# Attention scores from fp16 high and low parts in one 96-row contraction, with the next image's column scan and first turned tiles ahead of the first score

## What is computed

```python
Bx, Cx, Hx, Wx = x.shape
...
H, D = (6, 32)
WIN = 33
PAD = (WIN - 1) // 2
```

## Time and profile before

| | |
|---|---|
| median of the runs | 2979.17 us (2968.48 to 2982.03) |
| the profiled execution's own time | 2979.13 us |
| its span | 2977.3 us |
| PE busy | 2501.1 us (84%) |
| DVE busy | 1862.8 us (63%) |
| ACT busy | 1173.2 us (39%) |
| POOL busy | 810.9 us (27%) |
| fp32 score products, L1644 | 304.4 us, 704 instructions |
| mask products, L1647 | 118.6 us, 352 instructions |

### The profile page before, as it was taken

How to read it: one execution, slowest core, us unless ns; L and a number is a source line. 1 busy time by engine, 2 the same in 40 slices (tenths; PEclk the granted TensorE clock), 3 DMA queues, 4 the chain that set the end, 5 groups by cost and what they waited for, 6 DMA issues and landing times. The chain is left out here.

```text
span 2977.3 us, 50620 instructions
## 1 busy us (share of the span) xinstructions
PE 2501.1 (84%) x18147; PEld 1875.5 (63%) x18147; DVE 1862.8 (63%) x5249; ACT 1173.2 (39%) x3443; POOL 810.9 (27%) x656
## 2 busy tenths in 40 slices
PE   1349797889899899989898998989898998988697
PEld 0237575667676676767676776767676766766364
DVE  5346465766666665666676666656666666665454
ACT  0015343444443534444443435344443435353122
POOL 0000021323241313323232313233232413232444
PEclk9759697999999999899998999998999999998898
DMA  1540021334224233334333242433342242424664
GB/s 42 76 145 14 13 64 29 97 68 104 72 50 123 40 113 58 95 74 102 72 93 83 43 129 34 122 54 99 68 106 70 50 124 30 119 47 118 148 163 101
DMA packets 272442, 242.24 MB, mean 81 GB/s; under 512 B 208988, under 2 KB 250174, under 8 KB 261568
## 3 DMA queue, kind: packets, MB, share of 16 engines
q1 hardware_dynamic: 211456, 147.61, 18.5%
q0 software_dynamic: 50880, 52.59, 10.8%
q10 hardware_dynamic: 9856, 38.80, 4.1%
HBM read 133.73 MB, written 73.59 MB: 70 GB/s over the span
## 5 line engine op out<-in xcount | busy, mean ns | idle before, releaser
L1596 PE MATMUL PSUM<-XT,WB 128*128 128x512 f16 x2010 | 530.6, 397 | 22.7 <-DMA META<-slots 17.3
L740 POOL DMA_INDIRECT out_dram<-Y,META x228 | 359.0, 1575 | 565.8 <-DVE Y L1136 443.7
L886 ACT ACTIVATE PSPT<-PSUM,NMX 94x126 f32<-94x126 f32 x1056 | 367.1, 358 | 368.2 <-PE PSUM L1656 188.5
L854 ACT ACTIVATE HF<-PSUM,WB 128x512 f32<-128x512 f32 x402 | 274.1, 686 | 509.4 <-PE PSUM L1596 508.5
L1614 PE MATMUL PSUM<-WB,HHI 128*128 128x192 f16 x1608 | 403.4, 251 | 46.7 <-DVE HLO L1112 45.3
L1615 PE MATMUL PSUM<-WB,HHI 128*128 128x192 f16 x1608 | 402.2, 250 | 0.0
L1616 PE MATMUL PSUM<-WB,HLO 128*128 128x192 f16 x1608 | 402.0, 250 | 0.0
L1109 DVE TENSOR_SCALAR HHI<-HF 128x512 f16<-128x512 f32 x402 | 177.6, 442 | 328.5 <-ACT HF L854 326.5
L1596 PEld LDWEIGHTS PSUM<-XT,WB 128*128 128x128 f16 x2010 | 199.0, 102 | 189.9 <-issue 33.5
L1644 PE MATMUL PSUM<-KBD,QT 128*94 128x378 f32 x704 | 304.4, 516 | 9.1 <-ACT PSPT L886 7.5
L1112 DVE SCALAR_TENSOR_TENSOR HLO<-HF,HHI 128x512 f16<-128x512 f32 x402 | 278.4, 692 | 13.8
(11 more groups left out here) (276 smaller groups left out, 4412.6 us busy)
## 6 DMA issues: line engine op xcount, KB each, us to landing
WB<-weights SPq DMA_DIRECT2D x67, 1600.0 KB, 6.9
XR<-in_x ACTq DMA_DIRECT2D x16, 768.0 KB, 5.3
out_dram<-X ACTq DMA_DIRECT2D x32, 384.0 KB, 2.9
weights<-WB ACTq DMA_DIRECT2D x4, 1600.0 KB, 6.5
GUP<-TGU SPq DMA_DIRECT2D x256, 8.0 KB, 1.8
slots<-XROW,IDX POOLq DMA_INDIRECT x256
out_dram<-Y,META POOLq DMA_INDIRECT x228, 3.6
HF<-in_w ACTq DMA_DIRECT2D x6, 384.0 KB, 4.7
```

Source lines behind the costliest of these rows:

```text
L740: pool.indirect_dma_start(out[:, :], bass.IndirectOffsetOnAxis(row, 0), Y[:, wslot(i, j), q, :], None, bounds_check=B * T + BS - 1, oob_is ...
L854: act.activation(HF[:, k % 2, :], PSUM[:, 4 + k % 2, :], ACT.Gelu, scale=1 / (X_UP * W_UP), bias=bias).then_inc(f["gelu_done"], 1)
L886: e = act.activation(PS[0:QS, n % 2, h, :], PSUM[0:QS, n % 2, h * KS:(h + 1) * KS], ACT.Exp, bias=NMX[:, b, n % 2, h:h + 1], accum_out=DEN ...
L1596: mm = pe.matmul(dst, WB[:, ws, w:w + 128], XT[:, xs, chunk, :], start=(n == 0), stop=(n == 4))
```

## The change

Queries and keys are split into fp16 high and low parts. ACT writes the high part of each of the 12 pieces and, once more, the whole value in fp32 (WIDE); DVE subtracts one from the other and writes the low part. DVE takes all six value pieces. 36 DMAs for each image on SP (`spread`) then set, for every head, 32 rows of q high, q high, q low under each other (QS3) and k high, k low, k high (KS3), 96 rows in all, so that one fp16 product of 96 rows gives high x high + high x low + low x high. A tile becomes one mask product and three of 126 columns. The first two steps of the mix (`AHEAD = 2`) run ahead of block 0 on PE, ACT and DVE; the mix pairs keep their blocks, the rest of the mix comes one block earlier. PE waits for the last spread ahead of the first score.

```diff
-        KBD = sb("KBD", [128, 2, NB, HH, KS])
+        QS3 = sb("QS3", [128, HEADS, NB, QS], F16)
+        KS3 = sb("KS3", [128, HEADS, NB, KS], F16)
...
-        MIX_SLOT = [13, 15, 17, 19]
+        MIX_SLOT = [15, 17, 19, 21]
+        AHEAD = 2
...
+        def high_part(act, n):
...
+            for dst, ps in parts:
+                act.activation(dst, ps, ACT.Identity, bias=bias, scale=scale)
+            act.activation(WIDE[0:HC, n % 2, 0:width], src[:, 0:width], ACT.Identity, bias=bias, scale=scale
+                           ).then_inc(s["piece_act"], 1)
+
+        def low_part_of_piece(dve, n):
...
+            for dst, high, whole in parts:
+                last = dve.scalar_tensor_tensor(dst, whole, 1.0, high, ALU.mult, ALU.subtract)
+            last.then_inc(s["qk_low"], 1)
...
+            def spread(i):
+
+                for kind, dst, parts in (("q", QS3, (QPARTS[:, 0], QPARTS[:, 0], QPARTS[:, 1])),
+                                         ("k", KS3, (KHIGH, KLOW, KHIGH))):
+                    for oh in range(2):
+                        sp.wait_ge(s["qk_low"], at("qk_low", i, (6 if kind == "k" else 0) + 3 * oh + 3))
+                        for h in range(HH):
+                            for r in range(3):
+                                sp.dma_start(dst[r * HD:(r + 1) * HD, oh * HH + h, :, :],
+                                             parts[r][h * HD:(h + 1) * HD, oh, :, :]
+                                             ).then_inc(s[f"{kind}{oh}_spread"], 16)
...
                 if has(i + 2):
                     moves_in(i + 2)
+                if has(i + 1):
+                    spread(i + 1)
...
             def attention(i, stream):
                 before = not first(i)
                 side = (mix(i + 1),) if has(i + 1) else ()
-                pe.wait_ge(s["piece_act"], at("piece_act", i, PIECES // 2))
-                pe.wait_ge(s["piece_dve"], at("piece_dve", i, PIECES // 2))
+                step(side, AHEAD)
+                pe.wait_ge(s["piece_act"], at("piece_act", i, 12))
+                pe.wait_ge(s["piece_dve"], at("piece_dve", i, 6))
+                for kind in ("q0", "k0", "q1", "k1"):
+                    pe.wait_ge(s[kind + "_spread"], at(kind + "_spread", i, 16 * 9))
...
-                    pe.matmul(PSUM[0:QS, n % 2, 0:HH * KS], QT[:, oh, b, :],
-                              KBD[:, oh, b, :, :].rearrange("p h k -> p (h k)"), start=True, stop=False)
                     v = 0 if b == 0 else 2 if b == NB - 1 else 1
-                    pe.matmul(PSUM[0:QS, n % 2, 0:HH * KS], EYEB[:], MASKB[:, v, :], start=False, stop=True
-                              ).then_inc(s["score_done"], 1)
+                    pe.matmul(PSUM[0:QS, n % 2, 0:HH * KS], EYEB[:], MASKB[:, v, :], start=True, stop=False,
+                              skip_group_check=True)
+                    for h in range(HH):
+                        mm = pe.matmul(PSUM[0:QS, n % 2, h * KS:(h + 1) * KS], QS3[:, oh * HH + h, b, :],
+                                       KS3[:, oh * HH + h, b, :], start=False, stop=(h == HH - 1),
+                                       skip_group_check=True)
+                    mm.then_inc(s["score_done"], 1)
```

More of the change, by code:

```diff
@@ L280, in link @@
                         dve.wait_ge(dve_step, n_dve[0])
-                    for t in (XWF, KBD, XG, PSPT):
+                    for t in (XWF, QS3, KS3, XG, PSPT):
                         dve.memset(t[:], 0.0)
@@ L524, in hybrid_kernel, with widths @@
         act_engine = nc.scalar
-        def evacuate_piece(eng, n, give):
-            src = bank(n % 4)
-            is_act = eng is act_engine
+        def widths(n):
+            oh, (b0, b1) = n % 6 // 3, SPANS[n % 3]
+            return oh, b0, b1, (b1 - b0) * (QB if n < 6 else KS)
+        def high_part(act, n):
+            oh, b0, b1, width = widths(n)
+            src = bank(n % 4)[0:HC]
             if n < 6:
-                oh, (b0, b1) = n // 3, SPANS[n % 3]
-                k = b1 - b0
-                parts = [(QT[0:HC, oh, b0:b1, 1:QS], src[0:HC, 0:k * QB].rearrange("p (b q) -> p b q", b=k))]
+                bias, scale = BQS[:, oh:oh + 1], UNSCALE * HD ** -0.5
+                parts = [(QPARTS[0:HC, 0, oh, b0:b1, 1:QS], src[:, 0:width].rearrange("p (b q) -> p b q", q=QB))]
@@ L534, in evacuate_piece @@
                 if n % 3 == 2:
[L535 to L552, removed]
-            else:
[L554 to L561, removed]
@@ L562, in evacuate_piece @@
-            last.then_inc(give, 1)
+                    parts.append((QPARTS[0:HC, 0, oh, :, 0], src[:, width:width + 1].broadcast_to((HC, NB))))
+                    width += 1
+            else:
+                bias, scale = BK[:, oh:oh + 1], UNSCALE
+                parts = [(KHIGH[0:HC, oh, b0:b1, :], src[:, 0:width].rearrange("p (b q) -> p b q", q=KS))]
+            for dst, ps in parts:
+                act.activation(dst, ps, ACT.Identity, bias=bias, scale=scale)
+            act.activation(WIDE[0:HC, n % 2, 0:width], src[:, 0:width], ACT.Identity, bias=bias, scale=scale
+                           ).then_inc(s["piece_act"], 1)
@@ new lines, in low_part_of_piece @@
+        def low_part_of_piece(dve, n):
+            oh, b0, b1, width = widths(n)
+            wide = WIDE[0:HC, n % 2, :]
+            if n < 6:
+                parts = [(QPARTS[0:HC, 1, oh, b0:b1, 1:QS], QPARTS[0:HC, 0, oh, b0:b1, 1:QS],
+                          wide[:, 0:width].rearrange("p (b q) -> p b q", q=QB))]
+                if n % 3 == 2:
+                    parts.append((QPARTS[0:HC, 1, oh, :, 0], QPARTS[0:HC, 0, oh, :, 0],
+                                  wide[:, width:width + 1].broadcast_to((HC, NB))))
+            else:
+                parts = [(KLOW[0:HC, oh, b0:b1, :], KHIGH[0:HC, oh, b0:b1, :],
+                          wide[:, 0:width].rearrange("p (b q) -> p b q", q=KS))]
+            for dst, high, whole in parts:
+                last = dve.scalar_tensor_tensor(dst, whole, 1.0, high, ALU.mult, ALU.subtract)
+            last.then_inc(s["qk_low"], 1)
@@ L564, in hybrid_kernel, with evacuate_values @@
+        def evacuate_values(dve, n):
+            b0 = 2 * (n - 12)
+            k = min(2, NB - b0)
+            dve.tensor_scalar(VW[:, b0:b0 + k, :], bank(n % 4)[0:KS, 0:k * C].rearrange("p (b q) -> p b q", b=k),
+                              UNSCALE, None, ALU.mult).then_inc(s["piece_dve"], 1)
         O_COL = HH * QS
@@ L673, in _ @@
             moves_in(1)
+            spread(0)
             for i in range(B):
@@ L841, in pieces @@
                 windows(act.copy, 2, 1).then_inc(s["win_act"], 1)
-                for n in range(PIECES):
+                for n in range(12):
                     yield from slot.until(PIECE_SLOT + n)
-                    if n % 2 == 0:
-                        act.wait_ge(s["piece_done"], at("piece_done", i, n + 1))
-                        evacuate_piece(act, n, s["piece_act"])
+                    act.wait_ge(s["piece_done"], at("piece_done", i, n + 1))
+                    if n >= 2:
+                        act.wait_ge(s["qk_low"], at("qk_low", i, n - 1))
+                    high_part(act, n)
                 yield
```

40 lines of the change are left out of this document (26 added, 14 removed).

## The result

| | before | with the change |
|---|---|---|
| median of the runs | 2979.39 us (2968.48 to 2982.03, 4 runs) | 3026.08 us (3016.61 to 3037.40, 4 runs) |
| ratio, 95% interval | | **1.0166** (1.0138 to 1.0193) |
| profiled execution: time, span | 2979.13, 2977.3 us | 3037.40, 3035.6 us |
| granted clock, mean of the span | 0.922 | 0.868 |
| PE / DVE / ACT busy | 2501.1 / 1862.8 / 1173.2 us | 2490.1 / 1841.6 / 1227.8 us |

The kernel became slower by 47 us at the medians.

What follows compares the result with a forecast made beforehand. DVE was taken to bound the early blocks, PE those with a mix pair. Images 3 to 14 -10, images 0 to 2 +18, last image -5: +3 on 2979.13, 2982 us; range 2928 to 3030.

Steps and rivals of the forecast that it cites:

- no change: Whole kernel: the likeliest case, 2982 us, own range 2967 to 2994, no difference that can be told; chance 0.36.
- the rival of the low clock: Blocks 4 to 6: clock stays low through the first mix pair in every image, 3022 us; chance 0.20.
- Scores: PE's score tiles: mask plus three fp16 products 0.055 us apart, 0.33 us a score, 0.47 less than before.
- Start of attention: Last experts to first mix pair: 0.5 us less wait, PE idle 1.2, DVE 4.5 us late; gain of 1.1 us.
- Blocks with a pair: Three blocks with a mix pair: 5.36 us each instead of 5.85, 1.45 us in all.
- The clock, images 3 to 14: Blocks 2 to 5 into the first mix pair: clock drop costs 2.7 us, bounds 0 and 6; images sum to -10 us.
- near today's mean: Images 3 to 14: the choice of 2.7 us for the clock drop, today's mean being 3.0.
- Rival 2: Blocks 4 to 6: low clock lasts through the first mix pair, 6 us instead of 2.7, 3022 us; chance 0.20.
- Images 0 to 2: First score: no experts hide the spread, PE idle 6.8 us, +6 us each, +18 us in all.
- the low clock behind such a gap some 2 us: Images 0 to 2, behind PE's wait for the spread: slow clock adds some 2 us to the 6.8 us idle.
- Spread hidden in images 3 to 14: Before the first score: spread lands at 1010.7, ahead of 1015.4 when needed; costs nothing below 0.77 us a DMA.
- The last image: Attention without mix: blocks of 3.83 us, DVE's chain allows 3.0, in six blocks; -5 us.

Runs made afterwards that it cites:

- e1: The changed kernel plus four mask products with unread results ahead of the turns and of the values in blocks 1 to 5, images 0 to 14; 2979.00 us.
- e8: The changed kernel with 18 spread DMAs, unread products in blocks 1 to 5, and DVE's router comparisons moved ahead of the first tiles' statistics; 2958.76 us.
- e2: The changed kernel with only the first third of the spread, 12 DMAs an image instead of 36, the other rows left zero; 2990.18 us.
- e3: The changed kernel, fp16 scores kept, with the scan and all four turned tiles behind the first scores again, as in the kernel before; 3159.17 us.
- e12: The changed kernel with 18 spread DMAs and unread products in blocks 1 to 5, at each stage's end and in images 0 to 2's spread wait; 2934.78 us.

## Why the prediction was right, and where it was not

The time lies inside the range (2928 to 3030), near its upper end; "no change", the likeliest case, was wrong, and the rival of the low clock (3022 us, chance 0.20) came closest. Both are in part luck. The range was wide, and two of the four runs (3034 and 3037 us) lie above it. The rival had +30 us in images 3 to 14, where 15.6 were measured, and +18 in images 0 to 2, where 44.5 were: two errors of opposite sign.

- **Scores.** Forecast 0.33 us, products 0.055 apart; measured 0.33 (1065.65 - 1065.32) and 0.16 / 3 = 0.053. Right.
- **Start of attention.** Last Gelu 0.5 us earlier: the wait fell from 1.03 to 0.40. PE idle 1.2 us: 1.05. DVE idle 4.5: 4.59. With the clock held (e1) the block of the first pair ends 1063.71 - 1024.2 = 39.5 us behind the projections; forecast 1046.48 - 1.1 - 1006.2 = 39.2. Right, though not for DVE's sake, as e8 shows.
- **Blocks with a pair.** 5.36 us forecast, 5.35 measured.
- **The clock, images 3 to 14: the term that failed.** The forecast per stage was -3.5 us at full clock and +2.7 for one fall. e1 shows -2.7 (64.6 - 67.3, with whatever part of the idle work lies on the path) and the change +4.0 on top (68.6 - 64.6), so +1.3 instead of -0.8: 25 us over twelve images. The place was right, the first pair, and so was it that the low clock ahead of it is hidden (34.7 us to its block against 34.2 in e1). The price lay inside the bounds of 0 and 6; "near today's mean" was the wrong choice. The reason for a higher one stood in the forecast itself: PE loses work in just the blocks in which DVE kept it waiting. Rival 2 named the mechanism and priced it at 6.
- **Images 0 to 2: mis-sized too.** SP issued 36 in 23.9 us (forecast 22.9), the spread landed 25.6 us behind its start (25.2). The wait was 9.7, 8.6 and 9.5 us instead of 6.8; in image 1 PE was ready 17.0 us behind the spread's start (405.27 - 8.60 - 379.70) and not 18.4. Forecast +18, measured +44.5. Of the missing 26.5 us some 7 are the waits. Some 9 are "the low clock behind such a gap some 2 us", which is 5 by e2. And some 9 are the 2.5 us an image that scores and start were to gain: in e2, with no wait at all, the three stages take 190.0 us, 1.4 more than before instead of 7.5 less, and the clock falls there too (share 0.83 in image 1). The wait was priced nearly right, its consequence at two fifths, and the fall in mid-stage that images 3 to 14 were charged 2.7 us for was left out here.
- **Spread hidden in images 3 to 14.** Right: no wait for it; e3 shows what hides it, and what it would cost uncovered.
- **The last image.** -4.9 us in its attention (forecast -5), and +4.8 behind it, for the experts' tokens. The step that failed is to add a stage's gain without asking what is late next.

The sum: 26.5 + 25 + 5 - 1.7 (all else) = 55 us lie between the forecast +3 and the measured +58 of the profiled execution.

## What to carry to other kernels

Taking work off TensorE in blocks that wait for another engine can cost time in the next block, where TensorE is scarce: read the granted clock behind each wait, and price a wait as itself plus the slow stretch until the clock is back (waits of 27.9 us in sum cost 43.1 here). Where such waits can't go, products whose result nobody reads, put in front of them and kept shorter than the wait, are worth trying first: here they took 47 us off one kernel and 46 off another, and nothing where they lay on the path. And before a spread or gather is cut into fewer DMAs, look at both limits, the issues on the queue and the share of the DMA engines.

## What the runs showed of the hardware that was not expected

- The granted clock stayed at 1.2 GHz through stretches in which PE was 13.16 of 13.4 us busy, and in e3 through 47 us in which it was busy for 46.14: once low, a PE that was nearly always busy at half speed did not soon bring it back.
- Equal stages of one execution differ by where in them the clock falls: 67.7 to 71.3 us in images 3 to 14 of the changed kernel, 63.1 to 69.3 in e12. The four runs of the change spread over 21 us, from 3016.61 us at a mean granted clock of 0.877 to 3037.40 us at 0.868.
- 18 DMAs of 129 and 173 KB between partitions kept the DMA engines 0.84 busy at 182 GB/s (with an image load beside them), and the first score's wait still ended 4.7 us behind the last issue (393.41 - 388.71), where with 36 smaller ones it ended 1.65 us behind (405.27 - 403.62). An image load late in the spread did the same to 36 DMAs: 4.42 us in image 5 of e3.
